# Stack loads in four lots between the x loads, another order of front and first step, and neighbour counts in bf16 in a two-layer sequence kernel

## The reference

```python
# layer 0, for each row: causal_ema(b, tau) is h[t] = alpha(tau) * h[t-1] + b[t]
ctx = causal_ema(x, tau_ctx)
wg = sigmoid(concat([x, ctx]) @ Wg.T + bg)
gated = x * wg
h1 = gelu(x @ Wn1.T + bn1)
mod = 0.5 + sigmoid(h1 @ Wn2.T + bn2)                   # 32 modulations
traces = [causal_ema(gated * mod[..., d], tau_raws[d]) for d in range(32)]
temporal = einsum('dbtc,dc->btc', traces, softmax(blend, axis=0))
out = (gelu(x @ Wsoma.T + bsoma) * sigmoid(temporal @ Wtemp.T + btemp)) @ Wout.T
x = x + layernorm(out) * gamma + beta
# layer 1: 16 heads of 8 channels; a row takes the sparse or the dense form by u_prev
lam = 10 * exp(-5 * u_prev); use_sparse = lam >= 1
dense:  softmax(Q K^T * scale + lam * (prior_mask ? 0 : -1)) @ V
sparse: softmax over the 32 positions that prior_indices names (with repeats) @ V
x = x + where(use_sparse, sparse, dense) @ Wo.T + bo
```

## Time and profile before

| what | value |
|---|---|
| timed runs (median of 3) | 353.89 us (353.24 to 356.27) |
| the profiled execution | 351.38 us, span 349.6 us |
| busy over the span | PE 318.1 us (91%), DVE 290.8 (83%), POOL 224.9 (64%), ACT 214.6 (61%) |
| front and step 0 | 0 to 50.4 us |
| steps 1 to 5, from one `x1_ready` to the next | 20.9, 20.9, 20.5, 20.5, 21.2 us |
| step 6 and start of `end` | 154.4 to 174.9 us |
| from the first `scores` to the end of the span | 174.9 to 349.6 us |

### The profile page before, as it was taken

The page is one execution under the profiler, slowest core; times in us unless marked ns, Lnnn a source line. Parts: engine busy times, 40 slices in busy tenths (PEclk is TensorE's granted clock), DMA queues, the critical chain, the costliest instruction groups (busy, mean ns, idle before and its releaser), DMA issues. The chain is left out here.

```text
span 349.6 us, 10077 instructions
## 1 busy us (share of the span) xinstructions
PE 318.1 (91%) x3337; PEld 211.2 (60%) x3337; DVE 290.8 (83%) x1500; ACT 214.6 (61%) x458; POOL 224.9 (64%) x279
## 2 busy tenths in 40 slices
PE   8998698898989989898397889999999999999995
PEld 3553363554637455463253566777877777777774
DVE  4847899898998989897338966799999999999982
ACT  5760255464554546465504768888888888888873
POOL 2246445444453554535415697699999999999990
PEclk9998999999999999999969999999999999999999
DMA  6600011020200302015552043565546444401011
GB/s 182 194 2 1 30 34 60 2 67 24 62 30 2 92 1 62 30 41 95 94 105 62 1 77 94 78 104 136 137 98 121 102 115 100 102 5 33 2 33 32
DMA packets 29155, 23.08 MB, mean 66 GB/s; under 512 B 2736, under 2 KB 27824, under 8 KB 29104
## 3 DMA queue, kind: packets, MB, share of 16 engines
q1 hardware_dynamic: 29104, 22.44, 27.4%
HBM read 7.75 MB, written 2.10 MB: 28 GB/s over the span
## 5 line engine op out<-in xcount | busy, mean ns | idle before, releaser
L1546 POOL TENSOR_TENSOR arena<-arena,neg_max 128x512 f32<-128x512 f32 x128 | 129.6, 1042 | 22.4 <-DVE neg_max L1417 21.9
L1417 DVE CUSTOM_DVE_ANT_0 arena<-ps,arena 128x128 f32<-128x128 f32 x512 | 113.8, 286 | 10.9 <-PE ps L754 5.4
L1067 ACT ACTIVATE arena<-ps 128x512 f32<-128x512 f32 x128 | 69.6, 597 | 9.1 <-PE ps L768 9.0
L1494 POOL TENSOR_TENSOR arena<-arena 128x448 f32<-128x448 f32 (+6 forms) x56 | 41.2, 736 | 52.1 <-DVE arena L1255 48.9
L768 PE MATMUL ps<-ident_sb,arena 128*128 128x128 f32 x512 | 68.2, 276 | 0.0
L768 PEld LDWEIGHTS ps<-ident_sb,arena 128*128 128x128 f32 x512 | 56.5, 141 | 7.0 <-issue 5.3
L1417 DVE DVE_READ_ACCUMULATOR2_ANT neg_max<- 128x1 f32 x512 | 42.4, 83 | 0.2
L1481 POOL TENSOR_TENSOR arena<-decay_a,arena 128x192 f32<-128x192 f32 x32 | 20.6, 674 | 33.2 <-ACT arena L913 33.2
L784 PE MATMUL ps<-arena 128*32 128x128 f32 x1024 | 41.2, 279 | 0.0
L1255 DVE SCALAR_TENSOR_TENSOR arena<-ps,lag_c,arena 128x448 f32<-128x448 f32 (+6 forms) x56 | 25.8, 481 | 9.9 <-PE ps L517 5.8
L754 PE MATMUL ps<-arena 48*128 48x128 bf16 x512 | 25.6, 220 | 8.7 <-DMA arena<-k_parts 5.7
(11 more groups left out here) (166 smaller groups left out, 598.1 us busy)
## 6 DMA issues: line engine op xcount, KB each, us to landing
arena<-q_parts SPq DMA_DIRECT2D x96, 64.0 KB
arena<-k_parts SPq DMA_DIRECT2D x96, 64.0 KB
arena<-in_x SPq DMA_DIRECT2D x16, 256.0 KB, 3.0
arena<-in_xt SPq DMA_DIRECT2D x8, 256.0 KB, 2.8
out<-arena SPq DMA_DIRECT2D x7, 256.0 KB, 3.2
arena<-in_consts SPq DMA_DIRECT2D x1, 420.0 KB, 4.1
w_sb<-in_w SPq DMA_DIRECT2D x1, 384.0 KB, 5.8
w_sb<-in_w SPq DMA_DIRECT2D x1, 192.0 KB, 4.2
```

What stands on the lines that cost most here:

```text
L1067: act.activation(probT[q % PT_RING], ps[1][:, q % 2, :], ACT.Exp, scale=-1.0)\
L1417: dve.tensor_tensor_reduce(out=neg_t[q % NT_RING][:, cs], in0=ps[0][:, score_bank(c) + slot, cs], in1=nbias[n % 2], scale=1.0, scalar=3.0e ...
L1494: pool.tensor_tensor(a, a, pr_, ALU.add).then_inc(s["lag_added"], 1)
L1546: pool.tensor_tensor(t4, t4, neg_max[:, n % 2, 4 * z:4 * z + 4].unsqueeze(2).broadcast_to([P, 4, P]), ALU.subtract).then_inc(s["shifted"], 1)
```

## The change

Four things are edited.

- **SP.** The loop over `load_x` is written out, and behind the loads of groups 3, 4, 5 and 6 stand six transfers of stack 0 each: first and second half of q, then of k. `load_stack(0)` behind the loop goes. `idx` and `masks` are loaded after `ident`, no longer ahead of xT.
- **Front and step 0.** `f_context`, `f_modulation_n` and `f_gate_ctx` of group 1 move from `front` into `step(0)`, on PE and on ACT. In `front` `f_gated` goes ahead of `f_soma`, lags 2 and 3 follow it directly, and `value_bias` moves back. In step 0 `b_cross` comes ahead of `f_gate_ctx` and lags 0 and 1, and DVE's `b_locals` ahead of `f_mod_parts`. PE's warm-up has 10 matmuls in place of 14.
- **DVE's tables.** `early_tables` moves into the front between lags 1 and 2, the five conversions (`neighbours`) behind lag 3.
- **Counts.** `key_no` and the two running tables are bf16 (`so_far`); whole numbers up to 127 and counts up to 32 are exact in it. `FIRST_COUNT` gives step 0 six counts, step 1 six, and steps 2 to 5 five each. They stand two ahead of `b_temporal`, two ahead of `b_mixed` and the rest between lags 5 and 6. `late_tables` writes the sum to `lncnt`, and ACT waits for `cnt_none`.

```diff
@@ -28,7 +28,7 @@
 COUNTED = 6
-FIRST_COUNT = (0, 0, 7, 14, 20, 26, K_SPARSE, K_SPARSE)
+FIRST_COUNT = (0, 6, 12, 17, 22, 27, K_SPARSE, K_SPARSE)
 TERMS_Q = (0, 1, 0, 2, 1, 0)
@@ -128,7 +129,8 @@
         minus_ident_b = sb("minus_ident_b", [P, P], BF16)
-        key_no = sb("key_no", [P, P])
+        key_no = sb("key_no", [P, P], BF16)
+        so_far = [sb(f"so_far{k}", [P, P], BF16) for k in range(2)]
         table_probe = sb("table_probe", [P, 1])
@@ -313,12 +315,12 @@
                                    (c_sb, consts, "const_loaded"),
-                                   (idx_i[:], idx, "idx_loaded"), (masks_sb[:], masks, "idx_loaded"),
                                    (by_row(xT[0]), xt[:, 0:GB, :], "xT_loaded0"),
...
                                    (ident, ident_in, "ident_loaded"),
+                                   (idx_i[:], idx, "idx_loaded"), (masks_sb[:], masks, "idx_loaded"),
                                    (by_row(xT[1]), xt[:, GB:2 * GB, :], "xT_loaded1"),
@@ -341,14 +343,10 @@
-            with sp.Fori(0, G // 2 - 1) as i:
-                for m in (2, 3):
-                    load_x(i, m)
-            def load_half(g, which):
+            def load_half(g, which, first=0, last=NT):
                 parts, terms = ((q_parts, TERMS_Q), (k_parts, TERMS_K))[which]
-                for n, part in enumerate(terms):
+                for n, part in tuple(enumerate(terms))[first:last]:
                     for slot in range(2):
@@ -365,8 +363,13 @@
-            sp.wait_ge(s["part3_ready"], 2)
-            load_stack(0)
+            for r in range(2, G):
+                load_x(0, r)
+                if 3 <= r <= 6:
+                    sp.wait_ge(s["part3_ready"], 2)
+                    which, first = divmod(3 * (r - 3), NT)
+                    load_half(0, which, first, first + 3)
@@ -401,7 +404,7 @@
             pe.wait_ge(s["half_set"], 1)
-            for _ in range(14):
+            for _ in range(10):
                 pe.matmul(bank(1, 3), mod_pb[0][0:64, 0:P], mod_pb[0][0:64, :], start=True, stop=True)
@@ -427,6 +430,8 @@
                     pe.wait_ge(s["modT_tanh"], grp(i, m, 1, 1))
+                if at_start(i, m, 2) and not at_start(i, m, 1):
+                    pe.wait_ge(s["modn_ready"], 2)
                 four(ctx_bank(i, m), lambda cs: xn[u][:, cs], lambda cs: lt[:], "ctx_ps")
@@ -480,7 +485,8 @@
                 pe.wait_ge(s["modT_tanh"], grp(i, m, 1, 1))
-                pe.wait_ge(s["ctx_ready"], grp(i, m, 1, 1))
+                if not at_start(i, m, 2) or at_start(i, m, 1):
+                    pe.wait_ge(s["ctx_ready"], grp(i, m, 1, 1))
@@ -656,18 +662,14 @@
                 f_modulation(i, m + 1)
-                value_bias()
+                f_gated(i, m)
+                f_lags(i, m, range(2, 4))
                 f_soma(i, m + 1)
-                f_gated(i, m)
-                f_gate_x(i, m + 1)
-                f_lags(i, m, range(2, 3))
-                f_context(i, m + 1)
-                f_lags(i, m, range(3, 4))
                 b_carries(i, m)
                 f_lags(i, m, range(4, 5))
-                f_modulation_n(i, m + 1)
+                f_gate_x(i, m + 1)
                 f_lags(i, m, range(5, 6))
-                f_gate_ctx(i, m + 1)
+                value_bias()
                 f_lags(i, m, range(6, Q))
@@ -680,6 +682,11 @@
                 b_locals(i, m)
+                if not closes:
+                    f_modulation_n(i, m + 1)
+                    f_context(i, m + 1)
+                    b_cross(i, m)
+                    f_gate_ctx(i, m + 1)
                 if closes:
@@ -687,7 +694,7 @@
                     c_k(i, m - 1)
-                b_cross(i, m)
+                    b_cross(i, m)
                 f_gated(i, m + 1)
@@ -987,13 +994,15 @@
                 act.wait_ge(s["vec_step"], vec("lag_c"))
-                f_context(i, m + 1)
                 f_mod_part1b(i, m + 1)
-                f_modulation_n(i, m + 1)
-                f_gate(i, m + 1)
...
                 closes = not at_start(i, m, 1)
+                if not closes:
+                    f_modulation_n(i, m + 1)
+                    f_context(i, m + 1)
+                    b_cross(i, m)
+                    f_gate(i, m + 1)
                 if closes:
@@ -1017,7 +1026,7 @@
-                    act.wait_ge(s["vec_step"], vec("cnt_one"))
+                    act.wait_ge(s["vec_step"], vec("cnt_none"))
                     act.activation(lncnt[:], cnt1[:], ACT.Ln).then_inc(s["lncnt_ready"], 1)
@@ -1147,12 +1156,6 @@
                                                lna[:, 0:D].unsqueeze(1).broadcast_to([P, ND, D]), ALU.mult), waited=False)
-            pro("key_no", dve.tensor_copy(key_no[:], c_sb[:, C_K:C_K + P]), waited=False)
-            dve.wait_ge(s["idx_loaded"], 32)
-            pro("idx_f", dve.tensor_copy(idx_f, idx_i[:]), waited=False)
-            pro("mask_f", dve.tensor_copy(im_f, masks_sb[:, P:P + K_SPARSE]))
-            pro("idx_plus", dve.scalar_tensor_tensor(idx_m[:], idx_f, 1.0, im_f, ALU.add, ALU.mult))
-            pro("idx_masked", dve.tensor_scalar(idx_m[:], idx_m[:], -1.0, None, ALU.add), waited=False)
             dve.wait_ge(s["act_step"], scal("exp_blend"))
@@ -1180,7 +1183,17 @@
+            def neighbours():
+                pro("key_no", dve.tensor_copy(key_no[:], c_sb[:, C_K:C_K + P]), waited=False)
+                dve.wait_ge(s["idx_loaded"], 32)
+                pro("idx_f", dve.tensor_copy(idx_f, idx_i[:]), waited=False)
+                pro("mask_f", dve.tensor_copy(im_f, masks_sb[:, P:P + K_SPARSE]))
+                pro("idx_plus", dve.scalar_tensor_tensor(idx_m[:], idx_f, 1.0, im_f, ALU.add, ALU.mult))
+                pro("idx_masked", dve.tensor_scalar(idx_m[:], idx_m[:], -1.0, None, ALU.add), waited=False)
             def early_tables():
+                dve.wait_ge(s["w_rest_loaded"], 16)
+                dve.wait_ge(s["idx_loaded"], 32)
                 pro("w_out", dve.tensor_scalar(wt["wout"], wt["wout"], 0.5, None, ALU.mult), waited=False)
@@ -1197,20 +1210,20 @@
                 for j in range(first, last):
-                    so_far = (count_none, cnt1)[j % 2]
+                    n = so_far[j % 2][:]
                     if j < 2:
-                        pro(f"hot{j}", dve.tensor_scalar(so_far[:], key_no[:], idx_m[:, j:j + 1], None, ALU.is_equal),
+                        pro(f"hot{j}", dve.tensor_scalar(n, key_no[:], idx_m[:, j:j + 1], None, ALU.is_equal),
                             waited=False)
...
                         dve.wait_ge(s["vec_step"], vec(f"hot{j - 2}"))
-                        pro(f"hot{j}", dve.scalar_tensor_tensor(so_far[:], key_no[:], idx_m[:, j:j + 1], so_far[:],
+                        pro(f"hot{j}", dve.scalar_tensor_tensor(n, key_no[:], idx_m[:, j:j + 1], n,
                                                                 ALU.is_equal, ALU.add), waited=False)
...
                 dve.wait_ge(s["vec_step"], vec(f"hot{K_SPARSE - 1}"))
-                pro("count", dve.tensor_tensor(key_no[:], count_none[:], cnt1[:], ALU.add))
-                pro("cnt_one", dve.tensor_scalar(cnt1[:], key_no[:], 1.0, None, ALU.max), waited=False)
-                pro("cnt_none", dve.tensor_scalar(count_none[:], key_no[:], 0.0, BIG, ALU.is_equal, ALU.mult))
+                pro("count", dve.tensor_tensor(lncnt[:], so_far[0][:], so_far[1][:], ALU.add))
+                pro("cnt_one", dve.tensor_scalar(cnt1[:], lncnt[:], 1.0, None, ALU.max), waited=False)
+                pro("cnt_none", dve.tensor_scalar(count_none[:], lncnt[:], 0.0, BIG, ALU.is_equal, ALU.mult))
@@ -1334,7 +1347,10 @@
                 f_gated(i, m)
-                f_lags(i, m, range(0, 4))
+                f_lags(i, m, range(0, 2))
+                early_tables()
+                f_lags(i, m, range(2, 4))
+                neighbours()
                 b_carries(i, m)
@@ -1347,22 +1363,26 @@
                 first, last = FIRST_COUNT[2 * i + m], FIRST_COUNT[2 * i + m + 1]
-                half = (first + last) // 2
                 if closes:
...
                     c_residual(i, m - 1)
-                f_mod_parts(i, m + 1)
+                    f_mod_parts(i, m + 1)
                 b_locals(i, m)
+                if not closes:
+                    f_mod_parts(i, m + 1)
                 f_gated(i, m + 1)
                 f_lags(i, m + 1, range(0, 2))
-                if not closes:
-                    early_tables()
-                counts(first, half)
+                if first < last:
+                    counts(first, first + 2)
                 b_temporal(i, m)
                 f_lags(i, m + 1, range(2, 4))
-                counts(half, last)
+                if first < last:
+                    counts(first + 2, first + 4)
                 b_mixed(i, m)
-                f_lags(i, m + 1, range(4, 7))
+                f_lags(i, m + 1, range(4, 6))
+                if first < last:
+                    counts(first + 4, last)
```

(1 more changed line is left out.)

5 lines of the change are left out of this document (3 added, 2 removed).

## The result

The changed kernel takes 341.2 us (median; 340.3 to 341.9) where the kernel before, run beside it, takes 354.7 (353.2 to 356.3): a ratio of 0.961, 95% interval 0.956 to 0.966. The forecast was 341.1. Medians, ranges and ratios in this text leave out executions over 1.5% above the fastest of their kernel. The two profiled executions take 351.38 and 341.25 us, spans 349.6 and 339.3. (The profiled execution of before, 351.4, is shorter than all four that make its median.)

What follows compares the result with a forecast made beforehand. PE bounds the octets, PE and DVE nearly fill the steps, and a hole before `scores(0)` waits for late stack loads. Gains 8.3 + 4.5 + 0 + 0 = 12.8 us take 353.9 to 341.1 us; range 337.5 to 346.0.

Steps and rivals of the forecast that it cites:

- The hole: PE's wait before `scores(0)` for stack 0's loads, plus half clock behind it: 8.3 us won, bounds 5.7 to 8.6.
- Counts and DVE's order: Steps 1 to 5: fewer counts ahead of `b_mixed`, which then waits for the tanh; 4.5 us won, bounds 0 to 6.
- Rival 1: Hole goes but steps do not shrink, PE's work being the period or lags waiting for counts; 345.6 us, chance 0.16.
- Rival 5: Slower: all counts meet POOL's adds, growing to 1.08 us each on the path; 357.4 us, chance 0.02.
- Type: DVE's count tables in bf16: a count takes today's 0.34 us and today's waits, so no gain.
- Front and step 0: Reordered front and step 0 on PE, ACT and DVE: value taken 0, bounds -2.6 and +2.5 us.
- 1 us won at the front's end: Front term: 1 us gained at its end, with group 1's context, `modn` transposes and `gate_ctx` moved out.
- 2.1 us of early tables replaced by two counts (1.3): Step 0, DVE ahead of `b_temporal`: 2.1 us of tables leave, two counts of 1.3 us with POOL's wait come.
- 0.7 lost at `f_gated`: Step 0: group 1's moved context and `gate_ctx` matmuls, with ACT copies, precede `f_gated` and cost 0.7 us.
- Rival 4: Fewer warm-up matmuls and a thinner front leave PE slow longer in front and step 0; +4, 345.1 us, chance 0.05.
- a difference of 2.5 us from before to after: Timed median 353.89 us lies 2.5 above the profiled 351.38; the same difference was assumed for the changed kernel.
- slower rival: Rival 5: all counts held by POOL's adds and on the path; 357.4 us, chance 0.02.

Runs made afterwards that it cites:

- `hole_filled_34`: Kernel before with 34 useless matmuls on PE ahead of `scores(0)`, the wait for the stack staying; 351.75 us, one execution.
- `front_filled_full`: Changed kernel with 12 useless matmuls over all 128 partitions on PE in the front and step 0; 339.8 us (338.8 to 340.3).
- `after_again`: The changed kernel itself, unaltered, run again beside the first group of variants; 341.4 us (341.1 to 344.0), ratio 0.965 to the kernel before.
- `hole_filled`: Kernel before with 24 useless matmuls on PE ahead of `scores(0)`, the wait for the stack staying; 352.6 us, ratio 0.9965.

## Why the prediction was right, point by point

**The hole, 8.3 us: right, and for the reason given.** Measured 5.75 + 2.53 = 8.28 us in the profiled pair, and 8.28 with the lots alone. The half clock's part was shown apart as well, in the one trace of `hole_filled_34`. (The 3.0 us that the prediction gives for 14 repeats is a slip: 13 distances of 0.217 and one of 0.38 make 3.2, and 3.19 was measured.) Carries to locals: 4 us forecast, 4.11 measured; idle before `scores(0)` below 0.5: none.

**Counts and DVE's order, 4.5 us: right in the main, 0.6 short.** By step (the distance from T0 to the next add and so on) the gains are 0.15, 1.03, 1.36, 0.96, 0.95 and 0.70, sum 5.15. `b_mixed` waits for the tanh and the moments follow in 2.89 us, as said. From `b_temporal` to `b_mixed` steps 1 to 5 take 3.69, 3.70, 3.43, 3.42 and 3.43 us before and 2.59, 2.59, 2.73, 2.72 and 2.71 after: 4.33 us won, where 1.1 + 1.1 + 2.6 = 4.8 was forecast; steps 3 to 5 gave 0.71 each instead of 0.87. The remaining 0.8 us lie between a `b_mixed` and the next `b_temporal`, mostly 0.25 us each behind `b_mixed` of steps 2, 3 and 4, where one count fewer stands ahead of the next `b_temporal`. The prediction had said that this would add nothing; that it is this count is likely, no run separates it. Behind `b_mixed` of step 1, where two counts overrun, it is 0.07 us longer in all, for 0.3 forecast. Rival 1 (the steps do not shrink) falls: 19.17 us of PE's work now fit into 19.80. (Rival 5 read that the first count of a pair is never held by POOL; the earlier trace rows have one, at 80.94, that took 0.81 us.)

**Type: right, nothing.**

**Front and step 0, 0 us: wrong, +3.0 in the profiled pair, outside the +2.5 given as its bound.** The step had three terms. "1 us won at the front's end": DVE's locals start at 31.42 instead of 32.25, 0.83 won. "2.1 us of early tables replaced by two counts (1.3)": from `f_gated` of group 1 to `b_temporal` it is 3.26 us instead of 4.21, 0.95 won for 0.8 forecast. "0.7 lost at `f_gated`": between the start of the locals and `f_gated` it is 7.20 us instead of 2.40, 4.80 lost (4.80 - 0.83 - 0.95 = 3.02). That term failed, for two reasons. The moved matmuls were taken at their full-clock duration and as partly hidden, while they stand in one row on PE, with ACT copies between, ahead of the gate, and `b_cross` with them; at full clock that is 3.1 us between locals and `f_gated`, up to 0.9 of it fillers (`front_filled_full`). And the sum looked for a clock effect only in the warm-up, at the start, while the clock fell where PE's full-size work had been taken out of the front; that is the other 1.7 us. In the changed kernel all of PE's work from about 25.4 to 31 us is lags and locals with 32 partitions, and the clock is at half for some 10 us (27.2 to 37.4) instead of 3.5 (30.5 to 34.0). Rival 4 named this (a thinner front leaves PE slow for longer in the front and step 0) and was given a chance of 0.05; its price, +4, was that of a late rise at the start, and that did not happen: PE becomes fast at about 10 us in both traces. So what came was the forecast with a part of rival 4 in it. Whether ten warm-ups rather than fourteen cost anything was not tried by itself.

**From the profiled pair to the medians.** By the traces the sum is 10.3 us, and 351.4 - 10.3 gives 341.1 for the profiled execution; the forecast for that was 338.6. The median nevertheless came out as forecast, since the prediction carried a difference of 2.5 us from before to after, and the changed kernel's profiled execution lies at its median. In other words an error of 2.7 us was covered by a wrong assumption of 2.5 us: the total was hit by luck, the two gains were not. The larger set of executions beside `after_again` has the change at 12.1 us.

What makes the kernel before slower at its median than in its profiled execution is open in part. The wait for the stack varies: in `hole_filled`, which has the load order of before, SP issues the loads at the same distance from T6 as in the kernel before (the last ends 8.8 us behind it in both),

```profile
156.52 8.02 SPq L356 DMA_DIRECT2D arena<-q_parts  x12
164.59 7.83 SPq L356 DMA_DIRECT2D arena<-k_parts  x12
```

but `scores(0)` is released 5.9 us behind the last issue instead of 4.0, so it is the landing that came 1.9 us later. A wait that is gone cannot vary. Whether the extra matmuls of that variant delay the landing was not tried. The place of lag0 varies too, from 17.38 to 18.75 us in the four traces with the old front, but it does so with the changed front as well (16.96 to 18.29).

**Loads, octets, slower rival.** The lots cost nothing, the octets are unchanged (110.8 of 111 us busy), counts still meet POOL's adds (up to 1166 ns) but off the path.

## What to carry to other kernels

A wait at a place where an engine has nothing else can cost more than its length: here 5.75 us of idle TensorE brought 2.5 us of half clock behind it, and a load moved ahead won both. When matmuls are moved out of a stretch, price their new place as a chain, at both levels of the clock, and measure the granted clock of the stretch that they leave, even where the engine looks busy in it. When a difference between a profiled execution and the median is carried over, ask which wait makes it, and whether the change removes that wait. And when executions start at different times, compare distances from a marker behind the start.
